# Local attention scores: the mask added on VectorE with the row maximum, in place of mask products on TensorE

## The reference

```
# n = 1024 tokens, 8 heads of 64, windows of 64; bq, bk, bv: one window each
bk, bv = look_around(bk), look_around(bv)      # the window before and this one: 128 keys
sim = einsum('bhwid,bhwjd->bhwij', bq, bk)     # 64 queries x 128 keys per window and head
mask = (i < j) | (i > j + WINDOW) | (j == -1)
sim = where(mask, -finfo.max, sim)
attn = softmax(sim, axis=-1)
out = einsum('bhwij,bhwjd->bhwid', attn, bv)
...
x = x + o @ wo
h = layernorm(shift_token(x)) ; h = a * gelu(g) ; x = x + h @ w2 + b2
```

## Time and profile before

| | before |
|---|---|
| median of 3 runs | 2806.03 us |
| span of the profiled execution | 2805.7 us |
| PE (TensorE matmul) busy | 2684.9 us, 96% |
| ACT (ScalarE) busy | 2553.1 us, 91% |
| DVE (VectorE) busy | 2448.2 us, 87% |
| POOL (GpSimd) busy | 2145.0 us, 76% |

### The profile page before, as it was taken

One profiled execution on the slowest core, in us unless ns is written; L12 is line 12 of the kernel. 1 busy time (PEld: TensorE's weight loads), 2 busy tenths in 40 slices (PEclk: granted clock), 3 DMA queues, 4 the chain that ended last, 5 costly groups with the idle time before them and its releaser, 6 DMA issues.

```text
span 2805.7 us, 81380 instructions
## 1 busy us (share of the span) xinstructions
PE 2684.9 (96%) x31096; PEld 2285.2 (81%) x31096; DVE 2448.2 (87%) x6748; ACT 2553.1 (91%) x7853; POOL 2145.0 (76%) x2313
## 2 busy tenths in 40 slices
PE   5999999999999999999999999999999999999998
PEld 4788888888888888887777788888888888888886
DVE  7899999998888888886778999999998888888885
ACT  5999999999999999996444899999999999999996
POOL 7888888888888888883102888888888888888884
PEclk9999999999999999999999999999999999999999
DMA  4111111111111111110000111111111111111111
GB/s 109 35 45 32 30 24 30 26 27 32 26 30 32 30 26 28 30 23 11 8 1 10 26 30 34 30 23 30 26 26 36 23 36 30 37 35 31 37 31 29
DMA packets 64062, 84.00 MB, mean 30 GB/s; under 512 B 11794, under 2 KB 30908, under 8 KB 63676
## 3 DMA queue, kind: packets, MB, share of 16 engines
q1 hardware_dynamic: 63676, 78.82, 12.3%
HBM read 11.67 MB, written 4.19 MB: 6 GB/s over the span
## 4 chain that ended last, share of the span: by engine, by line
PE 43%; ACT 38%; DVE 14%; issue 2%; POOL 1%; SPq 1%; DMA 0%; ACTq 0%; DVEq 0%
ACT P L2751 15%; PE PS L671 4%; PE PS L661 4%; DVE SQ L1591 4%; DVE SS L1570 3%; PE PS L663 3%; PE PS L662 3%; PE PS L819 3%; ACT PT L2759 3%; PE PS L784 3%; PE PS L707 3%; DVE T L1582 3%; PE PS L724 3%; ACT G L2807 3%; ACT L2807 3%; ACT L2751 3%
## 5 line engine op out<-in xcount | busy, mean ns | idle before, releaser
L3389 POOL TENSOR_TENSOR T<-T,SQ 128x512 f32<-128x512 f32 x512 | 654.7, 1279 | 190.0 <-DVE SQ L1591 177.8
L2751 ACT ACTIVATE P<-PS,MX 128x128 f32<-128x128 f32 x2048 | 723.5, 377 | 11.8 <-DVE MX L1628 8.4
L3427 POOL TENSOR_TENSOR P<-P,RI 128x512 f32<-128x512 f32 x512 | 528.0, 1041 | 59.5 <-DVE RI L1635 57.4
L3403 POOL TENSOR_TENSOR T<-T,RN 128x512 f32<-128x512 f32 x512 | 527.3, 1046 | 2.1 <-DVE RN L1621 1.7
L2751 ACT ACTIVATION_READ_ACCUMULATOR P<-PS,MX 128x1 f32 x2048 | 441.7, 216 | 0.0
L661 PE MATMUL PS<-WH,YH 128*128 128x512 f32 x768 | 350.4, 456 | 21.0 <-POOL YL L3377 14.9
L1570 DVE TENSOR_REDUCE SS<-SQ 128x8 f32<-128x512 f32 x512 | 346.6, 678 | 9.8 <-ACT SQ L2702 9.5
L1628 DVE TENSOR_REDUCE MX<-PS 128x4 f32<-128x512 f32 x512 | 347.0, 678 | 5.7 <-PE PS L696 5.6
L724 PE MATMUL PS<-PT,VP 128*64 128x64 f32 x8192 | 294.7, 224 | 54.9 <-ACT P L2751 39.5
L724 PEld LDWEIGHTS PS<-PT,VP 128*64 128x64 f32 x8192 | 266.6, 138 | 95.5 <-issue 95.2
L2702 ACT ACTIVATE SQ<-PS 128x512 f32<-128x512 f32 x512 | 324.7, 635 | 20.0 <-PE PS L663 14.0
(11 more groups left out here) (135 smaller groups left out, 6986.2 us busy)
## 6 DMA issues: line engine op xcount, KB each, us to landing
VP<-VP SPq DMA_DIRECT2D x480, 128.0 KB, 2.3
out_dram<-X SPq DMA_DIRECT2D x32, 128.0 KB, 2.2
X<-in_L_attn_x_dram SPq DMA_DIRECT2D x7, 512.0 KB, 5.1
SG<-in_L_ffn_w_dram SPq DMA_DIRECT2D x5, 341.0 KB, 3.0
SG<-in_L_ffn_wqkv_dram SPq DMA_DIRECT2D x4, 384.0 KB, 3.5
SGQ<-in_L_ffn_wqkv_dram SPq DMA_DIRECT2D x4, 256.0 KB, 3.6
X<-in_table_dram SPq DMA_DIRECT2D x2, 512.0 KB, 6.1
P<-in_L_ffn_wo_dram SPq DMA_DIRECT2D x2, 256.0 KB, 4.2
```

Source lines behind the costliest of these rows:

```text
L2751: ins = act.activation(P[:, g, p, :], PS[:, b, 128 * p:128 * p + 128], ACT.Exp, bias=MX[:, g, p:p + 1], accum_out=SM[:, g, p:p + 1])
L3389: pool.tensor_tensor(T1[:, k, :], T1[:, k, :], SQ[:, (2 * n + 1 - x) % 3, :], ALU.add).then_inc(added[x], 1)
L3403: pool.tensor_tensor(heads, heads, RN[:, t % 2, i, 8 * x:8 * x + 8].unsqueeze(2).broadcast_to([128, HEADS, DH]), ALU.mult).then_inc(scaled ...
L3427: pool.tensor_tensor(P[:, g], P[:, g], RI[:, g, :].unsqueeze(2).broadcast_to([128, NPAIR, 128]), ALU.mult).then_inc(p_scaled, 1)
```

## The change

The four mask products per half step are gone, and the products of queries and keys start their own sums. The mask is kept in SBUF in float32 (`MSK`), for rows 0 to 63 in two variants (the second for the first window of a sequence). `row_max` becomes four fused operations, one for each pair: each reads the scores of 128 keys from PSUM and the mask from SBUF, writes minus their sum back to PSUM, and accumulates the minimum of that into a column of `MX`. The activations of `exp_rows` read the negated scores with scale -1.

```
-    MLOC = sb("MLOC", [2, 128], BF16)
+    MSK = sb("MSK", [2, 128])
...
-            for w in range(2):
-                v = 1 if first(t) and i == 0 and w == 0 else 0
-                for x in range(2):
-                    at = slice(64 * x, 64 * x + 64)
-                    pe.matmul(PS[64 * w:64 * w + 64, bank[f"S{2 * i + x}"], :], IDB[at, at],
-                              MLOC[at, v].unsqueeze(1).broadcast_to([64, NPAIR, 128]),
-                              start=True, stop=True)
...
-                                        QT2[at, s, p, m:m + WIN], KT[at, p, k:k + 128], start=False, stop=True,
-                                        skip_group_check=True)
+                                        QT2[at, s, p, m:m + WIN], KT[at, p, k:k + 128], start=True, stop=True)
...
-                dve.tensor_copy(MLOC[:, v], msk[:, c - C_KEEP:c - C_KEEP + 128]).then_inc(masks, 1)
+                dve.tensor_copy(MSK[0:64, v], msk[0:64, c - C_KEEP:c - C_KEEP + 128])
+                dve.tensor_copy(MSK[64:128, v], msk[64:128, C_LOC - C_KEEP:C_LOC - C_KEEP + 128]).then_inc(masks, 1)
...
-            dve.tensor_reduce(MX[:, g, :], PS[:, bank[f"S{g}"], :].rearrange("p (n k) -> p n k", n=NPAIR), AX.X,
-                              ALU.max, negate=True).then_inc(maxed, 1)
+            b, v = bank[f"S{g}"], 1 if first(t) and g < 2 else 0
+            for p in range(NPAIR):
+                at = slice(128 * p, 128 * p + 128)
+                ins = dve.tensor_tensor_reduce(PS[:, b, at], PS[:, b, at], MSK[:, v], -1.0, 3e38, ALU.add, ALU.min,
+                                               accum_out=MX[:, g, p:p + 1])
+            ins.then_inc(maxed, 1)
...
                 ins = act.activation(P[:, g, p, :], PS[:, b, 128 * p:128 * p + 128], ACT.Exp, bias=MX[:, g, p:p + 1],
-                                     accum_out=SM[:, g, p:p + 1])
+                                     scale=-1.0, accum_out=SM[:, g, p:p + 1])
```

## The result

The changed kernel takes 2921.15 us (median of four runs, 2918.91 to 2923.07) against 2807.46 us for the kernel before (now the median of four runs; the 2806.03 above was that of three): 1.0407 times, 95% interval 1.0392 to 1.0422, or 114 us more. The forecast of 2961 us had the right sign and was 40 us too high; the range of 2880 to 3190 us holds it.

What follows compares the result with a forecast made beforehand. Three engines were taken as nearly full; VectorE's longer maxima cost 1.45 us a step in layers 0 and 2, ScalarE's slip 0.97 in 1 and 3. 64 x (1.45 + 0.97) = 155 us on 2805.7: 2961 us, range 2880 to 3190.

Steps and rivals of the forecast that it cites:

- TensorE's relief turns into idle time.: Mask products before the scores: removing them frees TensorE 59 us, which becomes idle once another engine sets the step.
- One becomes eight, a pair costs 0.30 us.: VectorE's `row_max`: four fused operations and four accumulator reads, 1.20 us in place of 0.60, growth 2.40 us a step.
- the lower bound of 0.264: Least cost of a fused operation and its read on VectorE, 0.197 + 0.067 us; forecast with it 2907 us.
- the 0.264 to 0.34 us: Cost of a fused operation with its read on which the forecast's own range, 2905 to 3015 us, rested; chance 57%.
- Rival (a): VectorE's fused operations and reads don't overlap, 0.36 to 0.435 us a pair: 3040 to 3193 us; chance 25%.
- rival (b): VectorE's fused operation streams at half rate, 0.13 us more, 0.43 us a pair: 3190 us; chance 6%.
- The first pair lies on ScalarE's path.: Maxima of tiles 0 and 1 delay ScalarE's exponentials; it loses 0.97 us a step in layers 1 and 3.
- Layers 0 and 2: VectorE's work sets the step: VectorE needs 18.67 + 2.40 = 21.07 us a step there, 1.45 more than the step has.
- the same slip is below VectorE's 1.45: In layer 0 ScalarE's slip of 0.97 us is hidden below VectorE's excess of 1.45 us a step.
- the failed step: Maxima of tiles 2 and 3 were to push only VectorE, into its waits, delaying no other engine.
- The second pair of maxima pushes only VectorE, into waits that it has.: Maxima of tiles 2 and 3: exponentials start 0.94 and 1.69 us after them, so their growth delays only VectorE.
- loops through several engines: Sign that the forecast is wrong: such loops add slips outside the separate sums for VectorE's work and ScalarE's path; no size.

Runs made afterwards that it cites:

- no_mask: The kernel before without the mask products on TensorE and without any mask, row maximum still one reduction: 2809.82 us, 1.0016 times.
- mask_twice: The changed kernel with the mask products kept on TensorE as well, so the mask is added twice: 2923.76 us, 1.0420 times.
- both loops opened: The changed kernel with `y0_up` ahead of tile 3's maximum on VectorE and `project(s, 0, K)` ahead of `turn_p` on TensorE: 2893.10 us, 1.0310 times.
- second_pair: The changed kernel with only tiles 2 and 3 fused; tiles 0 and 1 keep mask products and the reduction: 2842.36 us, 1.0127 times.

## Why the prediction was right, and where it was off

- *TensorE's relief turns into idle time.* Right, and shown twice: 0 of 59 us without the change (no_mask), 0 with it (mask_twice).
- *One becomes eight, a pair costs 0.30 us.* The step was right, the size too high: 0.25, a little below the lower bound of 0.264. The read was taken from ScalarE's row at 0.10 us; on VectorE it costs 0.05, and between fused operations it is listed with the same start as the next one (849.81 both). So the pair lies outside the 0.264 to 0.34 us on which the forecast's own range rested, although the time lies in that range. Rival (a) is out: the read starts at 849.81, ahead of the end of its operation at 849.61 + 0.29. So is rival (b): 512 columns in 0.60 us is the full rate. The Trainium skill (VectorE: DVE Perf Modes, The DRAIN you can't avoid) has the next operation wait for an empty pipe, but adds that an operation that is not held starts earlier. This trace agrees with the second: behind reductions and fused operations the next one starts 0.08 us and more ahead of the end.
- *The first pair lies on ScalarE's path.* Right as a mechanism; its 0.97 us was too much because of the pair. With 0.25 a pair, known by then from the trace after, 0.56 us a step was worked out, and 0.59 and 0.55 were measured, 74 us in all.
- *Layers 0 and 2: VectorE's work sets the step, "the same slip is below VectorE's 1.45".* Wrong as a mechanism. With 0.25 a pair VectorE would need 18.67 + 1.40 = 20.07 us, but the step is 20.90 and VectorE idles 5% of it. (With both loops opened its own queue takes 20.39 us, so the 20.07 is also 0.32 too small; why wasn't found.) With its own rules and the right pair the forecast would have been 0.56 us in all 128 steps, 72 us, 2878 us. Of the 43 us that are then missing, 35 are the failed step (second_pair); the rest is about 2 us of the first pair and about 5 that the two pairs make only together:
- *"The second pair of maxima pushes only VectorE, into waits that it has."* True in layers 1 and 3 (19.53 us, no change), false in layers 0 and 2 (0.54 us, 35 us in all). The 0.78 us of waits were counted as if all of them lay behind the second pair and nothing else in the queue was waited for in between. `y0_up` and `y1_high` stand there, and in layers 0 and 2 the next projection needs both.

The two errors, 83 us too much for the pair (155 against 72) and about 43 too little for the loops, partly cancel. The forecast of 2961 us is nearer than its reasons deserve, and that is luck. Its last paragraph named loops through several engines as a sign that it would be wrong; that is what was seen.

Of what the profile after would show, the step of 21.1 and 20.5 us came out at 20.90 and 20.06, VectorE's busy time of 2755 us at 2632.9, and ScalarE's two waits for `MX`, 0.5 to 0.6 and 0.4 us, at 0.31 and a gap of 0.17. Two sums among the rivals are slightly off by the prediction's own rules: 0.43 a pair gives 3183 us, not 3190, and for 0.36 a pair ScalarE's path in layers 1 and 3 is the longer one (1.38 us against 1.24), so 3049 us, not 3040.

## What to carry to other kernels

On VectorE in this trace, an operation that accumulates a column per group is two instructions per group: count start to start, and ask whether one accumulation over the whole tile would do. An engine that is 98% busy is not for that the one that sets the step; take work from it and look for the wait that appears, as `no_mask` did here. Before an operation is lengthened "into a wait", list what stands between it and that wait in its queue, and who waits for each; where two loops run side by side, remove both before calling either harmless.

## What the hardware showed that I had not expected

- A read of VectorE's accumulator lasts 138 ns but delays the queue by only 0.05 us; behind a fused operation of 512 columns it delayed it by nothing that shows (808.32 to 808.92, 0.60 us, as for a reduction).
- The fused sum, write-back to PSUM and minimum ran at the rate of the plain reduction: 0.20 us for 128 columns and 0.60 for 512, start to start.
- TensorE's busy share moved from 98.1% to 96.0% in layer 1 when the mask products were taken away (no_mask, 431.88 of 450 us), with the step unchanged: a share near full did not mean that TensorE set the step.
